# A four-layer graph network: layer 0's three edge sums as one bf16 product of exact parts, layer 1's count product left out

## The reference

```python
h = (x @ W).reshape(n, H, C)                     # 4 heads of 32
alpha = leaky(a_src[src] + a_dst[dst])
m = segment_max(alpha, dst)
ex = exp(alpha - m[dst])
denom = segment_sum(ex, dst)
out = segment_sum(h[src] * (ex / denom[dst]), dst)   # layer 0
agg = segment_sum(dis[row] * dis[col] * h[row], col) # layer 1, deg by source
```

## Time and profile before

| | |
|---|---|
| median of 3 runs | 5755.3 us (5745.56 to 5755.92) |
| the profiled execution, own time | 5750.34 us |
| its span | 5748.5 us |
| mean granted TensorE clock | 0.714 |
| PE / weight loads / DVE / ACT / POOL busy | 76 / 62 / 63 / 30 / 68% of the span |
| layer 0's loop | 808 to 1541 us |
| layer 1's loop | 1702 to 2769 us |

### The profile page before, as it was taken

The page is one execution under the profiler, slowest core; times in us unless marked ns, Lnnn a source line. Parts: engine busy times, 40 slices in busy tenths (PEclk is TensorE's granted clock), DMA queues, the critical chain, the costliest instruction groups (busy, mean ns, idle before and its releaser), DMA issues.

```text
span 5748.5 us, 124694 instructions
## 1 busy us (share of the span) xinstructions
PE 4340.3 (76%) x26535; PEld 3551.3 (62%) x26536; DVE 3626.2 (63%) x10847; ACT 1734.3 (30%) x5601; POOL 3890.9 (68%) x3352
## 2 busy tenths in 40 slices
PE   3666549999729898989577777777773688888884
PEld 3555549999719888888455555555552455555553
DVE  5666775555665444444655555555554688888886
ACT  0000000000001111111266665666663244445442
POOL 4777787770016777777288888888885477777771
PEclk6555555555555555555699888889886899999997
DMA  5666535552123233223044444444444344445441
GB/s 122 193 188 188 163 105 164 163 164 75 46 75 84 78 77 77 78 76 77 20 35 36 35 35 36 35 35 36 35 36 79 107 135 134 134 134 135 133 134 40
DMA packets 396077, 536.69 MB, mean 93 GB/s; under 512 B 86434, under 2 KB 273900, under 8 KB 396001
## 3 DMA queue, kind: packets, MB, share of 16 engines
q0 software_dynamic: 213152, 301.19, 27.6%
q1 hardware_dynamic: 134897, 125.62, 7.2%
q10 hardware_dynamic: 47952, 109.14, 6.4%
HBM read 408.63 MB, written 127.00 MB: 93 GB/s over the span
## 4 chain that ended last, share of the span: by engine, by line
PE 25%; POOL 19%; issue 17%; DMA 17%; DVE 17%; ACT 3%; SPq 1%; DVEq 1%; ACTq 1%; POOLq 0%
POOL ACCB L460 12%; DMA acc_dram<-GR,ARENA 12%; PE WIDE L613 9%; POOL acc_dram L469 5%; DMA ARENA<-p_dram,SRCI 4%; PE WIDE L615 3%; DVE ACCB L1002 3%; POOL ARENA L486 2%; DVE ARENA L1184 2%; PE WIDE L724 2%; PE WIDE L549 2%; DVE ARENA L1002 2%; PE WIDE L706 2%; DVE T L1002 2%; DVE ARENA L1522 1%
## 5 line engine op out<-in xcount | busy, mean ns | idle before, releaser
L469 POOL DMA_INDIRECT acc_dram<-GR,ARENA x830 | 1283.2, 1546 | 349.1 <-ACT GR L812 221.7
L452 POOL DMA_INDIRECT GR<-h_dram,SRCI x830 | 911.9, 1099 | 327.4 <-issue 241.6
L486 POOL DMA_INDIRECT ARENA<-p_dram,SRCI x830 | 864.5, 1042 | 302.3 <-issue 154.8
L460 POOL DMA_INDIRECT ACCB<-h_dram,SRCI x830 | 805.1, 970 | 276.6 <-issue 251.7
L724 PEld LDWEIGHTS WIDE<-ACCB 128*128 128x128 f32 x3320 | 544.4, 221 | 390.5 <-issue 283.2
L724 PE MATMUL WIDE<-ACCB 128*128 128x128 f32 x3320 | 597.0, 310 | 234.9 <-issue 234.9
L651 PE MATMUL WIDE<-ACCB 128*128 128x128 f32 x1660 | 648.4, 494 | 122.7 <-DMA ACCB<-h_dram,SRCI 84.4
L1002 DVE TENSOR_TENSOR ACCB<-iota,DLC 128x640 f32<-128x640 f32 x332 | 274.7, 827 | 695.2 <-PE WIDE L653 377.9
L1431 DVE SCALAR_TENSOR_TENSOR ACCB<-WIDE,ARENA,ACCB 128x128 f32<-128x128 f32 x1660 | 567.7, 350 | 181.3 <-ACT ACCB L910 162.5
L613 PE MATMUL WIDE<-ACCB 128*128 128x128 f32 x1660 | 642.9, 491 | 33.6 <-DVE ACCB L1002 33.6
L1006 DVE TENSOR_SCALAR ACCB<-ACCB,SRC 128x128 f32<-128x128 f16 x832 | 291.1, 350 | 480.1 <-ACT ACCB L812 472.0
(11 more groups left out here) (317 smaller groups left out, 8046.5 us busy)
## 6 DMA issues: line engine op xcount, KB each, us to landing
T<-pairs_dram ACTq DMA_DIRECT2D x167, 320.0 KB, 3.8
g_dram<-GR SPq DMA_DIRECT2D x166, 320.0 KB
ACCB<-g_dram ACTq DMA_DIRECT2D x166, 320.0 KB, 3.0
ARENA<-src_rows_dram SPq DMA_DIRECT2D x166, 160.0 KB, 3.0
GR<-h_dram,SRCI POOLq DMA_INDIRECT x830
ACCB<-h_dram,SRCI POOLq DMA_INDIRECT x830, 2.5
acc_dram<-GR,ARENA POOLq DMA_INDIRECT x830
GR<-in_attr SPq DMA_DIRECT2D x830, 16.0 KB
```

The source lines that it names most:

```text
L452: pool.indirect_dma_start(GR[:, q, :], None, h_dram[:, :], row_of(j)).then_inc(landed[q], 16)
L460: pool.indirect_dma_start(GX[:, q, :], None, h_dram[:, :], row_of(j)).then_inc(l1_landed[q], 16)
L469: pool.indirect_dma_start(acc_dram[q % NACC][:, :], bass.IndirectOffsetOnAxis(ap=SCI[:, j:j + 1], axis=0), GR[:, q, :], None, compute_op=A ...
L486: pool.indirect_dma_start(HC3[:, j % RING3, :], None, p_dram[:, :], bass.IndirectOffsetOnAxis(ap=SRCI[:, j:j + 1], axis=0)).then_inc(lande ...
```

## The change

The nine f32 columns of a slot become 26 bf16 columns. Each of the four ex and the four maxima is written as a sum of three bf16 numbers (what bf16 holds of it, what bf16 holds of the rest, and the rest of that), which is 24 columns; two columns of ones replace the mark. The product L615 then is bf16, and it needs the one-hot in bf16: ACT casts it once a group into a new buffer OHB. DVE and ACT take turns in making the parts before the loop (REST is what is left after each part). After the loop DVE adds the three parts, and takes the count of edges per node from the columns of ones, CNT, which layer 3 uses; whether a node has an edge is min(CNT, 1). So layer 1's count product (L653) and the copy of CNT after it are left out. EXTP is moved in PSUM so that no slot's 26 columns cross a bank; the degree sum moves behind it.

```diff
+EXC = 3 * 2 * HEADS + 2
+EXT_AT = 7 * 512 - 14 * EXC
+DEG_AT = EXT_AT + NT * EXC
-        EXF = carve(ARENA, SPAD * 12, SPAD, 9)
+        EXF = carve(ARENA, SPAD * 13, SPAD, 2 * HEADS)
+        EXB = carve(ARENA[:, 0:SPAD * EXC // 2].bitcast(BF16), 0, SPAD, EXC)
+        REST = [carve(T12, SPAD * 4 * k, SPAD, HEADS) for k in range(2)]
+        OHB = carve(T12[:, HALF * P + HALF * NT + 3:2 * HALF * P + HALF * NT + 3].bitcast(BF16), 0, 2, HALF, P)
...
-            pe.matmul(bank(7, NT), identb[:, :], zerob[:, 0:1].broadcast_to([P, NT]), start=True, stop=False, skip_group_check=True
+            pe.matmul(bank(7), identb[:, :], zerob[:, 0:1].broadcast_to([P, 512]), start=True, stop=False, skip_group_check=True
...
-                pe.wait_ge(ev("l0_messages"), i * LONG + g + 1)
+                pe.wait_ge(ev("l0_onehot_cast"), i * LONG + g + 1)
+                pe.wait_ge(ev("l0_messages"), i * LONG + g + 2)
...
-                    pe.matmul(EXTP[:, t, :].rearrange("p a b -> p (a b)"), onehot,
-                              EXF[:, bass.ds(i * LRING + q, 1), :].rearrange("p a b -> p (a b)"),
+                    pe.matmul(EXTP[:, t, :].rearrange("p a b -> p (a b)"), OHB[:, h, k, :],
+                              EXB[:, bass.ds(i * LRING + q, 1), :].rearrange("p a b -> p (a b)"),
                               start=False, stop=False, skip_group_check=True)
-                    last = pe.matmul(bank(7, NT), LOA0[:, h, k, :], HIA0[:, h, k, :], start=False, stop=False,
+                    last = pe.matmul(DEGP, LOA0[:, h, k, :], HIA0[:, h, k, :], start=False, stop=False,
...
-                    counted = pe.matmul(EXTP[:, bass.ds(ts[k], 1), 0:1].rearrange("p a b -> p (a b)"),
-                                        OH01[:, h * HALF + k, :], ones[:, 0:1], start=False, stop=False, skip_group_check=True)
...
-            act.activation(EXF[:, :, 0:HEADS], ADAS[:, :, 0:HEADS], ACT.Exp).then_inc(ev("ex"), 1)
+            act.activation(EXF[:, :, 0:HEADS], EXF[:, :, 0:HEADS], ACT.Exp).then_inc(ev("ex"), 1)
+            act.wait_ge(ev("ex"), 1)
+            copy(EXB[:, :, 0:4], EXF[:, :, 0:HEADS]).then_inc(ev("ex_part"), 1)
+            act.wait_ge(ev("ex_rest"), 1)
+            copy(EXB[:, :, 12:16], REST[0]).then_inc(ev("ex_part"), 1)
+            act.wait_ge(ev("ex_rest"), 2)
+            copy(EXB[:, :, 8:12], REST[1]).then_inc(ev("ex_part"), 1)
...
+            def l0_cast(i, g):
+                h = g % 2
+                act.wait_ge(ev("l0_onehot"), i * LONG + g + 1)
+                copy(OHB[:, h, :, :], OH01[:, h * HALF:(h + 1) * HALF, :]).then_inc(ev("l0_onehot_cast"), 1)
...
             def l0_load(i, g):
...
                               ).then_inc(ev(f"l0_loaded{g}"), 16)
+                l0_cast(i, g)
...
-            link(v.tensor_copy(EXF[:, :, 8], FIRSTC))
...
-            link(tt(ADAS[:, :, 0:4], AS, MT, ALU.subtract))
+            link(tt(EXF[:, :, 0:4], AS, MT, ALU.subtract))
             made("ex_argument")
-            v.wait_ge(ev("ex"), 1)
+            link(v.tensor_copy(EXB[:, :, 4:8], EXF[:, :, 4:8]))
+            link(tt(REST[0], EXF[:, :, 4:8], EXB[:, :, 4:8], ALU.subtract))
+            v.sem_inc(ev("ex_rest"), 1)
+            link(v.memset(EXB[:, :, 24:EXC], 1.0))
+            v.wait_ge(ev("ex_part"), 1)
+            link(tt(REST[1], EXF[:, :, 0:4], EXB[:, :, 0:4], ALU.subtract))
+            v.sem_inc(ev("ex_rest"), 1)
+            v.wait_ge(ev("ex_part"), 2)
+            link(tt(EXB[:, :, 20:24], REST[0], EXB[:, :, 12:16], ALU.subtract))
+            v.wait_ge(ev("ex_part"), 3)
+            link(tt(EXB[:, :, 16:20], REST[1], EXB[:, :, 8:12], ALU.subtract))
+            v.sem_inc(ev("l0_messages"), 1)
...
-            link(v.tensor_copy(EXT[:, :, :], EXTP))
+            link(v.tensor_copy(CNT[:, :], EXTP[:, :, 24]))
+            link(v.tensor_copy(EXT[:, :, 0:8], EXTP[:, :, 0:8]))
+            for part in range(1, 3):
+                link(tt(EXT[:, :, 0:8], EXT[:, :, 0:8], EXTP[:, :, 8 * part:8 * part + 8], ALU.add))
...
-            link(v.tensor_copy(CNT[:, :], EXTP[:, :, 0]))
```

More of the change, by code:

```diff
@@ L60 @@
 BIG = 1e30
+EXC = 3 * 2 * HEADS + 2
+EXT_AT = 7 * 512 - 14 * EXC
+DEG_AT = EXT_AT + NT * EXC
+assert NT * D <= EXT_AT and DEG_AT + NT <= 8 * 512
 EPS = 1e-5
@@ L242, in gnn_stack @@
         whole_tiles_sum = stat[:, 2, :]
[L244 to L245 removed]
+        WIDE = ctx.enter_context(nc.psum_tensor("WIDE", [P, 8 * 512], F32))
+        LASTB = WIDE[:, 7 * 512:8 * 512]
         def bank(b, n=512):
[L248 removed]
+            return WIDE[:, b * 512:b * 512 + n]
         NODES = WIDE[:, 0:NT * D].rearrange("p (t f) -> p t f", f=D)
         SUMS = WIDE[:, 0:POSITIONS * HID].rearrange("p (t f) -> p t f", f=HID)
[L252 removed]
+        EXTP = WIDE[:, EXT_AT:EXT_AT + NT * EXC].rearrange("p (t f) -> p t f", f=EXC)
+        DEGP = WIDE[:, DEG_AT:DEG_AT + NT]
         def V(name):
@@ L650, in l1_sum @@
                     pe.wait_ge(l1_landed[q], i * 16 + (before_l1(q) + 16))
-                    pe.matmul(NODES[:, bass.ds(ts[k], 1), :].rearrange("p a b -> p (a b)"),
-                              OH01[:, h * HALF + k, :], GX[:, q, :], start=False, stop=False, skip_group_check=True)
-                    counted = pe.matmul(EXTP[:, bass.ds(ts[k], 1), 0:1].rearrange("p a b -> p (a b)"),
-                                        OH01[:, h * HALF + k, :], ones[:, 0:1], start=False, stop=False, skip_group_check=True)
+                    summed = pe.matmul(NODES[:, bass.ds(ts[k], 1), :].rearrange("p a b -> p (a b)"),
+                                       OH01[:, h * HALF + k, :], GX[:, q, :], start=False, stop=False, skip_group_check=True)
                     if k == GROUP - 1:
-                        counted.then_inc(ev("l1_sums"), 1)
+                        summed.then_inc(ev("l1_sums"), 1)
                     if k == 0:
@@ L1284, in l0_messages @@
                 tt(OH01[:, h * HALF:(h + 1) * HALF, :], iota[:, :].unsqueeze(1).broadcast_to(column),
-                   DLC[:, bass.ds(at, GROUP)].unsqueeze(2).broadcast_to(column), ALU.is_equal)
+                   DLC[:, bass.ds(at, GROUP)].unsqueeze(2).broadcast_to(column), ALU.is_equal).then_inc(ev("l0_onehot"), 1)
                 tt(LOA0[:, h, :, :], iotab[:, :].unsqueeze(1).broadcast_to(column),
@@ L1297, in _ @@
             v.wait_ge(ev("l0_sums"), GROUPS + LONG)
-            link(v.tensor_copy(DIS[:, 1, :], bank(7, NT)))
-            link(v.tensor_copy(EXT[:, :, :], EXTP))
+            link(v.tensor_copy(DIS[:, 1, :], DEGP))
+            link(v.tensor_copy(CNT[:, :], EXTP[:, :, 24]))
+            link(v.tensor_copy(EXT[:, :, 0:8], EXTP[:, :, 0:8]))
+            for part in range(1, 3):
+                link(tt(EXT[:, :, 0:8], EXT[:, :, 0:8], EXTP[:, :, 8 * part:8 * part + 8], ALU.add))
             EXL = SMN[:, 1, :, :]
-            link(ts1(HAS[:, :], EXT[:, :, 2 * HEADS], BIG, ALU.mult, -BIG, ALU.add))
+            link(ts1(HAS[:, :], CNT[:, :], 1.0, ALU.min))
+            link(ts1(HAS[:, :], HAS[:, :], BIG, ALU.mult, -BIG, ALU.add))
             link(tt(SMN[:, 2, :, :], EXT[:, :, HEADS:2 * HEADS], HAS[:, :].unsqueeze(2).broadcast_to([P, NT, HEADS]), ALU.add))
```

3 lines of the change are left out of this document (1 added, 2 removed).

## The result

The changed kernel takes 5708.2 us (median of 5 runs, 5698.9 to 5717.8); the kernel before takes 5755.3 beside it. The ratio is 0.9921, with a 95% interval of 0.991 to 0.9932: faster by 47 us, where 122 were forecast. 5708 lies above the range of 5585 to 5675.

The account below looks back on a forecast made before the run. Layer 0's loop was taken as bound by the array, then by PE's sequencer after the change, layer 1 by gathers. Terms -136 + 16 + 1 - 3 = -122 us from 5755.3 gave 5633 us, range 5585 to 5675.

Parts of the forecast that it names:

- The array: Layer 0's loop: a slot takes 0.667 us of array time instead of 0.88, a group of five slots 3.34.
- rival A: Layer 0's loop: the array is the bound, a group takes 3.34 to 3.45 us, the kernel 5593 to 5612; chance 25%.
- The exact parts: Ahead of layer 0's loop: ex_argument to first one-hot takes 21.1 us instead of 4.1; net +16 us (+13 to +18).
- The cast and the load behind it on ACT: Layer 0's loop: ACT's cast to bf16 and the next group's load queued behind it are hidden, costing nothing.
- What follows the loop: After layer 0's loop: three small PSUM reads and a minimum more, +1.1 us.
- the group of 3.58 us: Layer 0's loop: PE's sequencer sets the group at 3.58 us (3.34 to 3.75) instead of 4.40; gain 136 us (108 to 176).
- This is nearly all hidden: Layer 1's loop: removing L653 frees 354 us of array time, but gathers set the pace, so only -2.8 us.
- How gathers meet DVE's one-hots can move this by 8 us either way: Layer 1's loop: uncertainty of 8 us around the -2.8 us, from how gathers and one-hots meet.
- rival B: Layer 0's loop: gathers held by DVE run dry, below two a group; 5690 us, at worst 5742; chance 12%.
- C: Layer 0's loop: the load behind the cast makes it slower than before, 5847 us at a 9 us landing; chance 3%.
- D: Whole kernel: no gain that shows, from gathers at five in three groups and dearer exact parts; chance 2%.
- layer 1's loop within 10 us of 1067: Sign expected in the profile after: layer 1's loop nearly unchanged, PE idle more than a third, waiting for gathers.

Follow-up runs that it names:

- experiment 8: Changed kernel with fixed PSUM tile places in layer 0's sums, so PE loads no registers there: 5642.7 us, ratio 0.9823 to the kernel before.
- experiment 10: Changed kernel with layer 1's one-hot and layer 0's f32 one-hot each split into five one-input operations: 5619.9 us, ratio 0.977 to the kernel before.
- Experiment 2: Kernel before with only layer 1's count product left out (counts left zero): 5807.2 us, ratio 1.0105 to the kernel before.
- 1: Changed kernel with layer 1's count product put back, into free columns of PSUM bank 6, result unused: 5638.6 us, ratio 0.9815 to the kernel before.
- experiment 3: Changed kernel with layer 1's one-hot made by five operations of one SBUF input each: 5632.6 us, ratio 0.98 to the kernel before.
- 7: Changed kernel with 27 one-column memsets on DVE before each one-hot of layer 1: 5641.5 us, ratio 0.9799 to the kernel before.

## Why the prediction was wrong

*Right.* The array: a slot of 0.667 us. That PE's sequencer and not the array holds the group: rows and experiment 8 show it (rival A was a group of 3.34 to 3.45; the average is 3.68). The exact parts: 20.5 us for 21.1, in part because errors cancel: the cast to bf16 was priced 1.9 too high by a copy of f32 to f32, and DVE idled 0.55 for ACT and 0.43 ahead of the first one-hot. The cast and the load behind it on ACT are hidden: 4.5 us of waits in all. What follows the loop: +0.7 for +1.1.

*The term that was mis-sized* is the group of 3.58 us, which became 3.68: 17 us, a loop of 611 for 594. Two sizes in it were off, and they partly cancel. The rest of the sequencer's group (0.2, four steps of 0.39, the end, the wait) was taken as 2.35 us and measured as 2.18. And "1.23 for the load" put one load for all, where each group goes by its own, with the array's 3.34 as a floor. By that rule the loads of the kernel before would make 3.47 us a group, a loop of 576; entering their mean instead of the median would not have found the 3.68. But the loads themselves grew: those of over 1.3 us were 22 of 165 before and 64 after, the mean went from 1.17 to 1.35, the slowest from 2.09 to 2.44, and with these loads the rule makes 3.67. In both kernels they were longer while gathers ran (means of 1.22 against 1.08 before, 1.41 against 1.09 after), and in the shorter loop gathers, loads and stores move the same bytes in less time (161 GB/s in the stretch, 133 before). That this traffic makes the loads longer is likely, not shown; experiment 10 shows that a change of DVE's operations moves them too.

*The step that failed* is layer 1: "This is nearly all hidden [...] Sum -2.8 us", and "How gathers meet DVE's one-hots can move this by 8 us either way". It moved by +57. With layer 0's 17 us alone the time would have been 5650, inside the range; this step took it out. The mechanism had been named, and its price per hit was known (rival B used it for layer 0). The error was to treat the hits as chance that averages out. The bound of 8 us came from no count of how many gathers could be held. One in each of 166 groups by 0.43 us (the 1.37 for 0.94 of the earlier trace rows) is 71 us, and by the longest gather of the earlier trace rows, 1.58 us, 106; such a count would have covered what came. What decides is where the one-hot starts, and L653 stood just before that start in each of the 166 groups: removing hidden work of 0.43 us a slot started the one-hot 0.3 to 0.9 us earlier, and made its start even (2.59 to 2.67 us behind the last gather in the middle half, 2.92 to 3.54 before). So the conflict, once met, was met in nearly every group. Before, the gathers' asks in the last 146 groups were spread from ahead of the one-hot to its end, where a hold is short or none; after, 115 fell between 0.1 and 0.3 us behind its start, where 12 had. Experiment 2 reproduces the loss alone; 1, 3 and 7 each take it back, by a longer PE, another form of the operation, and a delay.

*Rivals.* B (gathers run dry) didn't happen: the gathers of layer 0 followed at 1.51 us, 2.45 a group instead of two, and the last started at 1330.8, 104 us before the last slot, where 15 to 25 were forecast. So the walk behind it, which held gathers through DVE's group, was too strict; which of DVE's four operations hold one, no run tests. C would have shown as DVE waiting for loads: 4.5 us. D: the gain is there. None of the rivals was the one that came true, a loss in layer 1; the listed sign "layer 1's loop within 10 us of 1067" is the one that failed.

What was forecast and what came: -136 became -119, +16 became +14 (the parts' 16.4, less 1.0 for the removed copy and 1.1 by which the unchanged stages ahead were shorter in this execution), +1 became +1, -3 became +57, and the unchanged rest gave +6. With layer 1's holds removed (experiment 3) the changed kernel takes 5632.6 us, by its ratio 5640. That this is the forecast of 5633 is partly luck: layer 1 is then 10 us better than forecast, and layer 0's loop 16 worse.

## What to carry to other kernels

Work that is hidden still sets the time at which something starts. Before leaving it out, ask what is released by its end, and whether that then falls on another engine's request at a shared resource; where both follow the same event, the answer is the same in every turn of the loop, so bound it by turns times the price of one hit. Then take the conflict away rather than tune the phase: here an operation form that doesn't hold the gathers, although it is slower by itself, is worth more than the timing. And where a sequencer sets the pace in some groups and the array in others, work group by group with the longer of the two: a short register load gives nothing back, and a long one is paid in full, so neither the median nor the mean of the loads is enough.

## What the runs showed of the hardware

- A gather (0.94 us on POOL) that asks while DVE runs an f32 `tensor_tensor` of two SBUF inputs waits for its end: 1.45 us, and 3.62 beside those of 3.9 us. In layer 1, before and after, a held gather ended 0.82 us after the one-hot did. It asked at least 0.06 us behind the one-hot's start; those that asked up to 0.03 us behind it, or ahead of it, took 0.94. Five `tensor_scalar` of 128 columns with one SBUF input (bf16 to f32) hardly hold it (0.94 to 1.02), and a memset of 128x448 does (1.74 together with the one-hot behind it). The Trainium skill, "SBUF — State Buffer", section "SBUF: two separate sides", says that the shared port is locked for the whole instruction, which these rows agree with; it says as well that two SBUF inputs count only against POOL work that reads SBUF. Whether that covers these gathers, which fetch rows from DRAM but have their indices in SBUF, the sentence leaves open; they do wait, so for them the exemption doesn't hold.
- Memsets of one column follow each other at about 0.015 us (27 in 0.39), and 27 in a row let a gather through.
- A load of five registers on PE takes 1.23 us with no gather running, but every fourth one 0.59; while gathers run it takes up to 2.44. DVE's form of the one-hot moves its mean (1.34 to 1.27). In a loop whose array time is 3.34 us a group, a group with a load above 1.3 us took that load and 2.18 us.
- DVE casts 128x3584 from f32 to bf16 in 2.03 us, half of what a two-input operation of that size takes (3.89).
